# A state-space block and a gated cumulative-sum layer in one kernel: the first batch's front alone, combined weights made among its scans, a new timetable

## The reference

```
h   = rmsnorm(layernorm(x)) @ w_in               # 256 -> 1024, split: xs, res (512 channels each)
xs  = silu(causal_conv4(xs));  res = silu(res)
delta, B, C = split(xs @ w_xproj)                # 16, 16, 16
delta = softplus(delta @ w_dt + b_dt)
h_n[t] = exp(delta[t] * A_n) * h_n[t-1] + delta[t] * xs[t] * B_n[t]     # n = 0..15
y   = sum_n h_n * C_n
x1  = x + layernorm(x + ((y + xs * D) * res) @ w_out)
# gated layer, two branches, 8 experts of rank 64 each
Q = xn @ W_Q.T;  K = xn @ W_K.T                  # second branch: times W_inv.T as well
prod = (Q @ V) * cumsum(K @ W)
gate = softmax(gelu(Q @ r1.T + b1) @ r2.T + b2 + expert_bias)
out  = ((prod * gate) @ U + gate @ b) / n_valid
result = x1 + layernorm((fwd + alpha * inv) @ W_O.T)
```

## Time and profile before

| | |
|---|---|
| median of 3 runs (2499.76, 2507.78, 4268.07) | 2507.78 |
| the profiled execution | 2508.51 |
| its span, first to last instruction | 2506.7 |
| busy: PE, DVE, ACT, POOL | 2175.4, 2185.3, 1845.7, 1857.7 |
| granted clock of PE, mean over the span | 0.929 |

### The profile page before, as it was taken

How to read it: one execution, slowest core, us unless ns; L and a number is a source line. 1 busy time by engine, 2 the same in 40 slices (tenths; PEclk the granted TensorE clock), 3 DMA queues, 4 the chain that set the end, 5 groups by cost and what they waited for, 6 DMA issues and landing times.

```text
span 2506.7 us, 35858 instructions
## 1 busy us (share of the span) xinstructions
PE 2175.4 (87%) x9268; PEld 1311.2 (52%) x9268; DVE 2185.3 (87%) x2820; ACT 1845.7 (74%) x3897; POOL 1857.7 (74%) x1324
## 2 busy tenths in 40 slices
PE   4666789899898989989898989989898998988787
PEld 2434546464554645555464646556464655646454
DVE  0389989898999989899898989999898999989931
ACT  4656686878878786887878787787868788785644
POOL 1668778787878878797877878787887878777620
PEclk9785899999998999999899999999999999999999
DMA  5111011111102011110101110110211111011100
GB/s 109 43 38 38 22 51 35 56 35 45 38 18 68 26 56 36 54 32 31 54 24 56 35 55 32 39 47 22 60 32 56 35 35 47 22 52 37 35 1 17
DMA packets 83400, 101.69 MB, mean 41 GB/s; under 512 B 23480, under 2 KB 49872, under 8 KB 83168
## 3 DMA queue, kind: packets, MB, share of 16 engines
q1 hardware_dynamic: 83168, 99.06, 13.1%
HBM read 90.13 MB, written 8.91 MB: 40 GB/s over the span
## 4 chain that ended last, share of the span: by engine, by line
PE 31%; DVE 27%; issue 19%; ACT 12%; POOL 5%; DVEq 1%; ACTq 0%; DMA 0%; POOLq 0%; SPq 0%
PE bank L758 18%; DVE h L1300 13%; DVE yT L1316 8%; PE stateT L931 7%; PE bank L906 3%; POOL bx L728 3%; ACT decay L1174 3%; ACT cum_sb L1139 2%; DVE xs L1211 2%; PE bank L892 2%; DVE yT L1313 1%; ACT rows L967 1%; DVE cumT L1255 1%; ACT scratch L1092 1%; DVE prod L1282 1%
## 5 line engine op out<-in xcount | busy, mean ns | idle before, releaser
L728 POOL TENSOR_TENSOR bx<-dx,B_rows 128x1024 f32<-128x1024 f32 x512 | 1199.9, 2363 | 229.5 <-DVE h L1300 197.6
L1300 DVE TENSOR_TENSOR_SCAN h<-decay,bx 128x512 f32<-128x512 f32 x1024 | 1240.1, 1211 | 83.3 <-ACT decay L1174 69.4
L1174 ACT ACTIVATE decay<-delta,decay_rate 128x512 f32<-128x512 f32 x1024 | 705.6, 693 | 316.7 <-DVE h L1300 315.2
L931 PE MATMUL stateT<-ident,h 128*128 128x128 f32 x4096 | 655.8, 293 | 209.0 <-DVE h L1300 126.8
L931 PEld LDWEIGHTS stateT<-ident,h 128*128 128x128 f32 x4096 | 497.6, 149 | 548.8 <-issue 294.6
L1316 DVE SCALAR_TENSOR_TENSOR yT<-stateT,C_tok,yT 128x512 f32<-128x512 f32 x960 | 698.1, 727 | 48.4 <-PE stateT L931 46.5
L758 PE MATMUL bank<-q_to_expert,xnT 128*128 128x512 f32 x512 | 264.4, 643 | 5.2 <-DVE xs L1211 5.2
L758 PE MATMUL bank<-k_to_expert,cumT 128*128 128x512 f32 x512 | 249.8, 611 | 11.6 <-DVE prod L1282 11.5
L1139 ACT ACTIVATE cum_sb<-bank,gate 128x64 f32<-128x64 f32 x1024 | 222.4, 326 | 32.7 <-PE bank L758 30.9
L758 PE MATMUL bank<-hT,w_in_sb 128*128 128x512 f32 x512 | 244.3, 607 | 1.7 <-ACT scratch L1030 0.9
L906 PE MATMUL bank<-expert_to_out,prodT 128*128 128x256 f32 x1024 | 241.3, 379 | 0.5 <-ACT cum_sb L1139 0.5
(11 more groups left out here) (168 smaller groups left out, 2615.1 us busy)
## 6 DMA issues: line engine op xcount, KB each, us to landing
B_rows<-B_scratch SPq DMA_DIRECT2D x256, 256.0 KB, 3.2
x_front<-in_L_attn_x SPq DMA_DIRECT2D x16, 512.0 KB, 5.2
x_back<-in_L_attn_x SPq DMA_DIRECT2D x16, 512.0 KB, 3.6
out<-x_back SPq DMA_DIRECT2D x16, 512.0 KB, 3.2
w_in_sb<-in_L_attn_w_in SPq DMA_DIRECT2D x1, 1024.0 KB, 5.9
h<-in_L_ffn_V_fwd SPq DMA_DIRECT2D x2, 256.0 KB
h<-in_L_ffn_W_inv_exp SPq DMA_DIRECT2D x2, 256.0 KB
h<-in_L_ffn_W_fwd SPq DMA_DIRECT2D x2, 256.0 KB
```

The costliest lines, as they stand in the source:

```text
L728: pool.tensor_tensor(bx[use % BX_RING][:, :, :], dx[q.parity][:, 2 * half:2 * half + 2, :], row, ALU.mult).then_inc(s_bx.step(f"{n},{half} ...
L931: last = pe.transpose(stateT[j % 2][:, c * P:(c + 1) * P], h[n % 2][:, c, j * P:(j + 1) * P], ident[:, :])
L1174: act.activation(decay[c % 2][:, :], delta[q.parity][:, c, :], ACT.Exp, scale=decay_rate[:, c, n:n + 1]).then_inc(s_exp.step(f"{n},{c}"), 1)
L1300: dve.tensor_tensor_scan(h[n % 2][:, c, :], decay[c % 2][:, :], bx[(2 * n + c // 2) % BX_RING][:, c % 2, :], 0.0, ALU.mult, ALU.add).then_ ...
```

## The change

- SP loads the front's own weights (w_in, norm, the convolution's, w_xproj, w_dt, b_dt) first, on a semaphore of their own, `front_ld`. PE waits for it at the first xs, ACT at the first hT copy. A_log's exp and DVE's constants move to beat 24 of the turn q = -1.
- The 22 jobs move into the turn q = 0, the scans of batch 0. They use the four rotating banks at beats at which a bank is free: at least 3 beats apart, from beat 1. ACT's copy follows 6 beats behind PE's step. The staged weights lie in tiles that B and L use later (cum_sb, prod, xnT, prodT, cumT, x_back, rows), and the transposes overwrite their sources. The waits for `w_act` = 22 move from the first scan step to SP's first x_back (issued at slot 15 for batch 0, no longer 12), PE's first rt and DVE's first r.
- The order of the jobs: W_Q W_inv and W_K W_inv come after branch 0.
- POOL's bx of a half waits only for the dx of its two blocks. The fourth dx moves from beat 127 to 128, thus behind bx of slot 0, half 0, and `keep` behind it.
- Many tasks get other beats. The convolution's split, two blocks on DVE and two as products on ACT with sums on POOL, stands already in the kernel before.

Cut to its core:

```diff
-JOBS_FROM, JOBS_EVERY = 60, 3
+JOBS_FROM, JOBS_EVERY = 1, 3
+KEPT_AFTER = 6
+READ_WITHIN = 14
+LATE = 24
...
-    ("B", "keep", "pool"): (255,),
+    ("B", "keep", "pool"): (258,),
-    ("F", "hT", "pe"): (18, 25),
+    ("F", "hT", "pe"): (17, 19),
-    ("F", "x", "sp"): (93,),
+    ("F", "x", "sp"): (80,),
-    ("F", "dt", "act"): (89, 89, 106, 112),
+    ("F", "dt", "act"): (89, 91, 106, 117),
-    ("B", "y", "pe"): (265, 265, 265, 265),
+    ("B", "y", "pe"): (263, 263, 265, 265),
-    ("B", "wo", "pe"): (279, 281, 282, 287),
+    ("B", "wo", "pe"): (279, 283, 283, 285),
-    ("B", "logit_rows", "pe"): (347,),
-    ("B", "lb", "dve"): (345,),
+    ("B", "logit_rows", "pe"): (343,),
+    ("B", "lb", "dve"): (342,),
-    ("B", "sub", "pool"): (355,),
+    ("B", "sub", "pool"): (352,),
-    ("F", "dx", "pool"): (103, 111, 126, 127),
-    ("L", "x", "pool"): (479, 480),
-    ("L", "store", "sp"): (477,),
+    ("F", "dx", "pool"): (108, 111, 126, 128),
+    ("L", "x", "pool"): (478, 482),
+    ("L", "store", "sp"): (461,),
...
             def period(q):
                 for at in range(BEATS):
                     scan_part(q, at // 8, at % 8)
+                    beat = at if name == "pe" else at - KEPT_AFTER
+                    if job_part and q.turn is None and q.const == 0 and beat in job_beats:
+                        i = job_beats.index(beat)
+                        place = job_banks[i]
+                        before = held[place]
+                        job_part(i, Use(bank[place], ...))
+                        if name == "pe":
+                            held[place] = (JobSteps, q, i)
...
-        stage_V = [h[0][:, 0:2, :], h[0][:, 2:4, :]]
+        stage_V = [cum_sb, prod]
...
-        job_bank = decay + stateT
-        job_beats = [JOBS_FROM + JOBS_EVERY * i for i in range(len(jobs))]
+        def bank_is_free(at, place):
+            return (not any(place == b and at - READ_WITHIN <= beat < at + KEPT_AFTER + 2 for beat, b in fills)
+                    and not any(place == b and at < beat + KEPT_AFTER + 2 for beat, b in zip(job_beats, job_banks)))
+        job_beats, job_banks = [], []
+        for at in range(JOBS_FROM, BEATS - KEPT_AFTER):
+            if len(job_beats) < len(jobs) and (not job_beats or at >= job_beats[-1] + JOBS_EVERY):
+                free = [place for place in range(4) if bank_is_free(at, place)]
...
             def load_x_back(batch):
+                if batch.turn is None and batch.const < 2:
+                    sp.wait_ge(w_act, len(jobs))
...
-                    if slot == 12:
+                    if slot == (NS - 1 if q.turn is None and q.const == 0 else 12):
                         load_x_back(q)
...
-                if q.turn is None and q.const == 0 and n == 0 and half == 0:
-                    pool.wait_ge(w_act, len(jobs))
-                if n == 0 and half == 0:
-                    pool.wait_ge(f_pool.sem, f_pool.done(q, "dx3"))
+                if n == 0:
+                    pool.wait_ge(f_pool.sem, f_pool.done(q, f"dx{2 * half + 1}"))
...
-                pe.wait_ge(w_ld, 16 * N_WEIGHTS[0])
                 pe.wait_ge(w_pool, 2)
...
             def xs_task(b, c, use):
+                if b.turn is None and b.const == 0 and c == 0:
+                    pe.wait_ge(front_ld, 16 * N_FRONT[0])
...
             def prologue():
                 act.preload_act_table_set(EXP_SET)
+
+            def rates():
                 act.wait_ge(w_ld, 16 * N_WEIGHTS[0])
                 act.activation(decay_rate[:, :, :], decay_rate[:, :, :], ACT.Exp).then_inc(w_rate, 1)
...
-                if q.turn is None and q.const == -1 and 8 * n + beat in job_beats:
-                    keep_combined(job_beats.index(8 * n + beat))
+                if q.turn is None and q.const == -1 and 8 * n + beat == LATE:
+                    rates()
```

More of the change, by code:

```diff
@@ L371, in bank_of, with done, walk @@
             return (uses_a_period * ((batch.const + 1 + periods) % 2) + use) % 4
-        def walk(engine, name, prologue, tasks, scan_part):
+        class JobSteps:
+            sem = w_act
+            @staticmethod
+            def done(batch, i):
+                return i + 1
+        def walk(engine, name, prologue, tasks, scan_part, job_part=None):
             beats = plan(name)
@@ L416, in walk @@
                 period(Batch(q))
-        stage_V = [h[0][:, 0:2, :], h[0][:, 2:4, :]]
[L420 to L423, removed]
+        stage_V = [cum_sb, prod]
+        stage_W = [[xnT[:, 0, :], xnT[:, 1, :]], [prodT[:, 4 * t:4 * t + 4, :].rearrange("p a b -> p (a b)") for t in range(DT)]]
+        stage_U = [[cumT[:, 0, :], cumT[:, 1, :]], [x_back[0][:, 2 * t:2 * t + 2, :].rearrange("p a b -> p (a b)") for t in range(DT)]]
+        wq_raw, wk_raw, winv_raw, wo_raw = (place[:, 2 * i:2 * i + 2, :] for place in (rows, x_back[1]) for i in range(2))
         r1_raw = o_rows[:, 0:2, :]
@@ L426, in program @@
         b_raw = o_rows[0:2 * KE, 3, :]
[L427 to L430, removed]
+        winvT, r1T, woT, wqiT, wkiT = winv_raw, r1_raw, wo_raw, wq_raw, wk_raw
+        bT = gate[:, 0:2, :]
         bias_raw = logits
@@ L744, in combine_weights @@
                     pe.wait_ge(e_ld, 16 * N_EXPERT[0])
-                if max(i - 3, depends + 1) > 0:
-                    pe.wait_ge(w_act, max(i - 3, depends + 1))
+                if use.sem is not w_act:
+                    pe.wait_ge(use.sem, use.free_at)
+                needed = max(depends + 1, use.free_at if use.sem is w_act else 0)
+                if needed > 0:
+                    pe.wait_ge(w_act, needed)
                 for mm in mms:
@@ L750, in combine_weights @@
                         k = src.shape[0]
-                        last = pe.transpose(job_bank[i % 4][:, mm[0]:mm[1]], src, ident[0:k, 0:k])
+                        last = pe.transpose(use.bank[:, mm[0]:mm[1]], src, ident[0:k, 0:k])
                     else:
-                        last = pe.matmul(job_bank[i % 4][0:parts, mm[0]:mm[1]], mm[2], mm[3], start=mm[4], stop=mm[5])
+                        last = pe.matmul(use.bank[0:parts, mm[0]:mm[1]], mm[2], mm[3], start=mm[4], stop=mm[5])
                 last.then_inc(w_pe, 1)
@@ L836, in rt_task @@
                 br, m = k // 2, k % 2
+                if k == 0 and b.turn is None and b.const == 0:
+                    pe.wait_ge(w_act, len(jobs))
                 if k == 0:
@@ L911, in scan_part @@
             def scan_part(q, slot, beat):
-                if q.turn is None and q.const == -1 and 8 * slot + beat in job_beats:
-                    combine_weights(job_beats.index(8 * slot + beat))
                 if beat % 2:
@@ L920, in scan_part @@
                     return
-                if j == 0 and n == 0 and batch.turn is None and batch.const == 0:
-                    pe.wait_ge(w_act, len(jobs))
                 if j == 0:
@@ L1184, in prologue, with constants @@
             def prologue():
+                pass
+            def constants():
                 dve.wait_ge(w_rate, 1)
@@ L1285, in scan_part @@
                 k = beat // 2
+                if q.turn is None and q.const == -1 and 8 * slot + beat == LATE:
+                    constants()
                 if beat % 2 == 0:
```

143 lines of the change are left out of this document (79 added, 64 removed), and 8 rows, old and new, of the table TIMETABLE.

## The result

| | before | after |
|---|---|---|
| median of 4 runs each, us | 2505.9 | 2468.4 (2463.2 to 2472.0) |
| ratio, 95% interval | | 0.9857 (0.9833 to 0.9881) |
| span of the profiled run | 2506.7 | 2461.4 |
| first scan | 101.7 | 69.2 |
| scans of batch 0, to the first of batch 1 | 132.2 | 134.2 |

The account below looks back on a forecast made before the run. It took DVE to bound the later batches, with the front as idle time to cut. From 2508.5: front -33.2, batch 0's scans +8, new beats 0, giving 2483.3, or 2483 from the median; range 2460 to 2508.

Parts of the forecast that it names:

- The front: Before the first scan: sums start at 4.3 and product copies leave, so the first scan comes at 68.5, 33.2 earlier.
- The products: Batch 0's scans: the 22 products moved there, together with the later fourth dx, cost +8; bounds -4 and +31.
- Beats 18 and 21: Batch 0's scans: products placed there run at clock 0.5 and make DVE wait, +4.
- its 3 or the 8 of the rows: Batch 0's products: cost some 3 by the skill's clock rule alone (2478), against 8 from the profile rows.
- 138 to 143 behind it: Sign of a right forecast: batch 1's first scan comes 138 to 143 after batch 0's first scan.
- 0 per batch, between -1 and +1: Later batches: the reordered beats change nothing, 0 per batch, times 14.
- the first rival: Later batches: the new beats take 2 off each of 14, -28, giving 2455; chance 0.13.
- later batches at 144 to 146: Sign of a right forecast: each later batch takes 144 to 146.
- The edges: Five loop edges: new order frees bx, but PE is as late as before, so 0; at best -1 each.
- B rows late: Rival, batches from the third on: row 13 misses POOL behind the store; 2518 at 2.5 a batch; chance 0.09.
- Half clock among the scans: Rival, batch 0: products run at half clock and cost 31, not 8; 2506, no change; chance 0.13.
- The front does less: Rival: something else holds the front's start to 15.7 and only the copies leave; 2495; chance 0.12.

Follow-up runs that it names:

- experiment 3: The changed kernel with the 22 products back in the front, every third beat from 60, early load and new beats kept: 2482.3, ratio 0.9926.
- experiment 1: The changed kernel with the timetable of the kernel before, early front and products among the scans kept: 2478.4, ratio 0.9912.
- experiment 2: The kernel before with the new timetable alone, bx of slot 0 waiting for its own half: 2490.4, ratio 0.9956.
- experiment 5: The changed kernel with ACT waiting for all small weights before the front's sums, as before the change: 2487.4, ratio 0.9952.
- experiment 7: The kernel before with two unread matmuls at the start of slot 10 of each batch, in PE's pause: 2474.7, ratio 0.991.
- experiment 10: The changed kernel with two unread matmuls at the start of slot 10 in all batches but batch 0: 2444.7, ratio 0.9772.
- experiment 4: The changed kernel with two unread matmuls of 512 columns at the start of slot 10 of every batch: 2447.4, ratio 0.9785.

## Why the prediction was right, and where it was not

**The front was right**, step by step: first sum 4.10 (4.3), table load 35.47 (35.7), projection 38.81 and 5.3 long (39.1 and 6.2), its copy 44.15 (45.3), softplus 46.02 to 61.08 (47.2 to 62.0), first scan 69.2 (68.5); 32.5 earlier for 33.2. The steps after softplus came out 8.1 for 6.5: POOL began its first of them at 62.18, 1.1 after ACT's end, since it was still at the channel block before; its addition and its bx began while DVE's products of line L1264 ran (1.74 each) and took 1.59 for 1.26 and 2.78 for 2.35. That is 1.1 + 0.3 + 0.4 = 1.8, less the hand-offs that I had; it takes more than the 0.9 by which softplus had ended early (61.08 for 62.0). What the prediction did not ask is how the two parts of this gain share it: alone the early load gives 7 (experiment 3), for the products would have stood in its way.

**The products were mis-sized**: batch 0 cost +2.0, not +8. Term by term, from the waits by beat: dx +1.3 (1.2). Beats 18 and 21 +2.0 in one wait (4): the first product runs at half clock, 3.22, the second already in 1.88. Ten products from 47 to 81: no wait for PE over 0.3 before beat 84 (2), at the clock of 1.00 that I had set for them; 0.9 and 0.6 at beats 84 and 86 stand in place of the 1.5 of before. From 89 on +0.5 for PE and 2.5 for ACT at beats 108 and 112 (3). And the wait of 4.1 at beat 36 is gone where I took off 2. The reason that I gave for it, a busier PE, is wrong: experiment 1 has the products with the old beats and keeps 4.0 there, experiments 2 and 3 have the new beats without the products and wait 0.7 at most. The new beats took it away, and in batch 0 I had not priced them. At equal beats the products cost 3.5 to 5.0 (134.2 against 130.7 and 129.4 with the new ones, 137.3 against 132.2 with the old), and the new beats gave back 1.5 to 3.1; each is a difference of single executions, where equal code gave 132 to 137. The half clock at batch 0's end is broken up (0.80 over beats 80 to 127), so the rule of the Trainium skill (TensorE: Matmul & The Clock Gate, Part 1), by which activity lifts the clock, had the clock right. Which cost was nearer, its 3 or the 8 of the rows, is not decided: the sum measured is 2.0, but products and dx at equal beats are 4.8 to 6.3. My sign "138 to 143 behind it" was missed: 134.2.

**The new beats: the step "0 per batch, between -1 and +1" failed in its mechanism.** The change was -1.1 a batch, just outside, and the first rival (the beats win 2 in each batch) is not what happened either. I treated the later batches as a fixed 144.8 to which the order adds or takes. Odd batches differ by 2.9 to 3.5 with the clock at beats 82 to 88, and the earlier trace rows held it: the 2.3 for PE and about half of a 0.62 in the 4.4 for ACT are the price of the fall. I read the clock of 0.95 as high. Experiments 5 and 7 show that in batches of equal clock the order gives next to nothing: 2025.1 against 2022.3 with falls, 1988.3 against 1989.1 without. What the change did is to let some falls go, and the new beats have a part in that: the profiles with the old beats and the pause unfilled have fourteen falls (before) and fourteen, three short (experiment 1), those with the new beats ten, ten and nine (after, experiments 2 and 3) and fourteen (experiment 5), and experiment 2 is faster than before by more than its interval. So the beats are worth something on average, by a way that I did not have. My sign "later batches at 144 to 146" was missed: their mean is 143.4.

**The edges were right** in the number, 0, and not in the reason: I had bx freed there, but DVE still waits for bx at the starts of batches 4, 6, 8, 10 and 12, 1.5 to 2.1 each (9.3 in all for 8.9).

**B rows late** did not come: no wait of POOL's shows in DVE's account beyond those edges. **Half clock among the scans** did not either. **The front does less** is refuted by the sum at 4.10.

**The total** lay in the range because the front, 32.5 of it, was worked out right. The other two terms were off by 6 and 15 (by the profiled pair), both to the fast side, and the range was wide enough for both; that part is luck.

Open: what decides that a batch gets the fall. The pause is in all, the profile with the whole shifted by 10.3 had it in fourteen of fourteen, experiments 2 and 3 had ten and nine; no run here varied the shift finely, and one execution of the same kernel can differ from the next by 9 (after) or 17 (before). Nor is it settled why two matmuls cost 11 more over fourteen batches than one (1977.1 and 1988.3; by the medians on one chip 9, 2435.9 and the 2444.7 of experiment 10). The second adds 0.77 of PE time a batch (31.7 against 19.3 over sixteen), 10.8 over fourteen, but DVE does not wait for it there: experiment 4 has no wait for PE between beats 82 and 94. Of the 11, waits for PE at other beats are 5.5, waits for ACT 1.7, and DVE is itself busy 4.4 longer (1906.3 and 1901.9). What starts the half-clock stretches behind batch 0's spread is open too.

## What to carry to other kernels

When identical loop rounds differ in length in one profile, split them by the granted clock at the instruction that the bound engine waits for, before costing any reordering; else the difference is credited to the edit. If TensorE pauses just ahead of matmuls that are waited for, try one matmul into the pause, sized to fit it, and try each further place by itself: here more places cost more than they gave. Profile more than one execution before counting such falls: here the number very likely changed from one to the next. And undo a change of two parts one part at a time: the early load and the moved products gave 32.5 together, and the load alone 7.

## What the runs showed of the hardware

- The same instructions, in a loop, were granted full clock in some rounds and half in others; a round with the fall (batch 7) took 145.3, one without (batch 5) 142.3, at equal busy time of DVE.
- A pause of 1.5 to 1.6 of TensorE stands ahead of every such fall in the kernels before and after, and ahead of the batches without one as well. One unread matmul (1.12) in it left one fall, a short one, of ten: 30.1 less over the fourteen batches.
- A clock of 0.99 bought with fifteen unread matmuls a batch is worse than 0.96: 2060.0 against 2007.2.
- Of DVE and POOL, the one that began second was the longer for it. DVE's 128x512 product of line L1264 has a median of 0.68 over 64, and took 1.74 the four times in the front, each begun 0.1 behind a POOL operation. That POOL operation kept its 1.27 (62.18), while the addition that began during the DVE product (63.53) took 1.59 for 1.26.
